# Attention sums of a graph kernel: from float32 products to two float32r products of an exact split

## The reference, cut to what matters

```python
e = leaky_relu(xl[src] + xr[dst], 0.2)
logits = einsum('ehc,hc->eh', e, att)
m = segment_max(logits, dst)
p = exp(logits - m[dst])
denom = segment_sum(p, dst)
out = segment_sum((p / denom[dst])[:, :, None] * xl[src], dst)
x = bn(leaky_relu(out.mean(axis=1) + bias, 0.01) + x)
```

## Time and profile before

| | us |
|---|---|
| median of 3 runs | 5818.48 |
| lowest, highest | 5813.25, 5839.03 |
| profiled execution, its own time | 5812.7 |
| its span, first to last instruction | 5811.0 |
| mean granted TensorE clock, share of full | 0.941 |

### The profile page before, as it was taken

The page is one execution under the profiler, slowest core; times in us unless marked ns, Lnnn a source line. Parts: engine busy times, 40 slices in busy tenths (PEclk is TensorE's granted clock), DMA queues, the critical chain, the costliest instruction groups (busy, mean ns, idle before and its releaser), DMA issues.

```text
span 5811.0 us, 137953 instructions
## 1 busy us (share of the span) xinstructions
PE 5019.3 (86%) x47293; PEld 3476.8 (60%) x47293; DVE 3747.3 (64%) x7195; ACT 1756.4 (30%) x3748; POOL 3820.1 (66%) x3980
## 2 busy tenths in 40 slices
PE   5999999788878888589999985999999859999997
PEld 4777777788868888345555553555555525555555
DVE  6566554888778888556665564566666746556666
ACT  3222222555530000133333322333333233333331
POOL 4777776676637776477777735777777267777770
PEclk8999899899889999899999997999999989999998
DMA  4655554332223333244444432444444234444442
GB/s 115 175 171 166 166 172 143 87 94 84 83 73 93 99 88 88 63 119 125 121 126 126 123 93 65 125 124 123 122 126 126 74 80 126 124 125 126 121 125 63
DMA packets 689966, 663.36 MB, mean 114 GB/s; under 512 B 398323, under 2 KB 480698, under 8 KB 689274
## 3 DMA queue, kind: packets, MB, share of 16 engines
q1 hardware_dynamic: 557482, 489.13, 27.6%
q0 software_dynamic: 127424, 164.72, 13.2%
q10 hardware_dynamic: 4368, 0.70, 0.1%
HBM read 564.89 MB, written 89.17 MB: 113 GB/s over the span
## 4 chain that ended last, share of the span: by engine, by line
PE 57%; issue 16%; POOL 16%; DVE 7%; DVEq 2%; DMA 1%; ACT 1%; ACTq 1%; POOLq 0%
PE ps L1059 18%; PE ps L904 13%; POOL rows L369 11%; PE ps L998 8%; POOL rows L382 5%; PE ps L1019 4%; PE ps L1033 3%; PE ps L919 2%; PE ps L1009 2%; PE ps L984 2%; PE ps L978 1%; DVE acc L1619 1%; DMA rows<-table,idx 1%; DVE region L1782 1%; DVE acc L1807 1%
## 5 line engine op out<-in xcount | busy, mean ns | idle before, releaser
L382 POOL DMA_INDIRECT rows<-table,idx x2340 | 2251.6, 962 | 1108.2 <-issue 710.2
L1059 PE MATMUL ps<-region,hot 128*128 128x272 f32 x4992 | 1314.3, 408 | 171.6 <-DVE region L1760 85.4
L1059 PEld LDWEIGHTS ps<-region,hot 128*128 128x128 f32 x4992 | 916.3, 193 | 466.9 <-issue 291.0
L666 ACT ACTIVATE region<-ps 128x512 f32<-128x512 f32 x1248 | 677.7, 596 | 1674.7 <-PE ps L998 1674.7
L1807 DVE TENSOR_TENSOR acc<-acc,ps 128x272 f32 x1248 | 544.5, 436 | 870.4 <-PE ps L1059 765.9
L904 PE MATMUL ps<-hot,region 128*128 128x192 bf16 (+1 forms) x9216 | 927.5, 261 | 81.1 <-DVE region L1634 56.4
L904 PEld LDWEIGHTS ps<-hot,region 128*128 128x128 bf16 x9216 | 846.5, 104 | 99.4 <-DVE region L1634 61.5
L369 POOL DMA_INDIRECT rows<-table,idx x728 | 699.9, 961 | 259.1 <-issue 221.0
L1782 DVE TENSOR_TENSOR region<-ps,region 128x1056 f32<-128x1056 f32 x582 | 724.9, 1252 | 45.9 <-issue 40.4
L998 PE MATMUL ps<-xT,wcat 64*128 64x512 f32 x2496 | 710.8, 646 | 9.3 <-ACT region L666 9.2
L402 POOL DMA_INDIRECT rows<-table,idx x448 | 429.9, 960 | 206.7 <-issue 120.7
(11 more groups left out here) (304 smaller groups left out, 6470.0 us busy)
## 6 DMA issues: line engine op xcount, KB each, us to landing
hot<-hot_dram SPq DMA_DIRECT2D x624, 256.0 KB
turned<-turned_dram SPq DMA_DIRECT2D x624, 128.0 KB
rows<-table,idx POOLq DMA_INDIRECT x3516
hot_dram<-hot SPq DMA_DIRECT2D x104, 512.0 KB
region<-hot_dram SPq DMA_DIRECT2D x96, 512.0 KB
xwin<-table SPq DMA_DIRECT2D x1664, 24.0 KB
region<-r_dram SPq DMA_DIRECT2D x109, 256.0 KB, 5.9
region<-d_dram SPq DMA_DIRECT2D x104, 256.0 KB
```

What stands on the lines that cost most here:

```text
L382: pool.indirect_dma_start(rows[:, n % 2, j, :], None, table, bass.IndirectOffsetOnAxis(ap=idx[:, s:s + 1], axis=0)).then_inc(rows_in3[n % ...
L666: act.activation(rz[g % 2][:, 2 * t + side, :], ps[:, Z + side, :], ACT.Relu).then_inc(rz_made, 1)
L1059: mm = pe.matmul(ps[:, sum_bank(k, side, i), 0:PC + H], hot[:, b, 4 * side + 2 * i + j, :], px[b][:, 4 * side + 2 * i + j, :], start=(j == ...
```

## The change

For groups below `TAIL` the weighted rows are made in float32 in one buffer `pxf` (the place of the old px[1]). ACT writes them rounded to float32r into `pxh` (`high_half`), DVE subtracts that from pxf and writes the rest to `pxl` (`low_half`), for each side of 128 x 4 x 272. The columns with the maxima are treated alike (`ends_half`; `low_ends` where a chunk begins). PE multiplies `hotr`, a float32r name for the memory of hot, by pxh and by pxl and adds both up in PSUM. pxf, pxh and pxl have one buffer for each side, so weigh of a side now waits for that side's sums of the group before. The last eight groups keep their two float32 buffers and their code. Some semaphores that nothing used are gone, and hot and region1 are placed first in memory; pxh lies where px[0] was, and pxl is a float32r name for the memory of pxf, so the subtraction is in place.

```diff
+        hotr = nc.alloc_sbuf_tensor_at("hotr", [P, 2, 8, P], F32R, offset=hot_at)
+        pxh = nc.alloc_sbuf_tensor_at("pxh", [P, 2, 4, 272], F32R, offset=region1_at)
+        pxl = nc.alloc_sbuf_tensor_at("pxl", [P, 2, 4, 272], F32R, offset=region1_at + 4 * 8 * 272)
...
+        pxh32 = pxh[:, :, :, :].bitcast(F32)
+        pxf = o1[:, 8 * 272:16 * 272].rearrange("p (a j c) -> p a j c", a=2, j=4)
...
+            def ends_half(k, side):
+
+                act.wait_ge(att_summed, 4 * (l * G + k - 1) + 2 * side + 2)
+                act.activation(pxf[:, side, :, PC:PC + H], ends_of(k)[:, side, :, :], ACT.Copy).then_inc(pm_made, 1)
+
+            def high_half(k, side):
+
+                n = PC if k % 8 == 0 else PC + H
+                act.wait_ge(wx_made, 2 * (l * TAIL + k) + side + 1)
+                if k % 8 != 0:
+                    act.wait_ge(pm_made, 2 * (l * G + k) + side + 1)
+                act.activation(pxh[:, side, :, 0:n], pxf[:, side, :, 0:n], ACT.Copy).then_inc(ph_made, 1)
...
                     weights_of(8 * done)
+                    if 8 * done < TAIL:
+                        high_half(8 * done, 0)
                 if u < G:
                     leaky(u, 0)
+                if phase == 2 and 0 <= done < CHUNKS and 8 * done < TAIL:
+                    high_half(8 * done, 1)
                 k = u + 1 - LAG
-                if 0 <= k < G and k % 8 != 0:
+                split = 0 <= k < TAIL and k % 8 != 0
+                if split:
+                    ends_half(k, 0)
+                elif TAIL < k < G:
                     weights_of(k)
                 if u < G:
                     leaky(u, 1)
+                if split:
+                    high_half(k, 0)
...
                     keep(u + 1)
                     turn(u + 1)
+                if split:
+                    ends_half(k, 1)
+                    high_half(k, 1)
...
-                    pe.wait_ge(pm_made, l * G + k + 1)
+                    if k < TAIL and k % 8 == 0:
+                        pe.wait_ge(fl_made, l * (CHUNKS - 1) + k // 8 + 1)
+                    elif k >= TAIL:
+                        pe.wait_ge(pm_made, 2 * (l * G + k) + 2)
...
+                            for part in (pxh, pxl):
+                                mm = pe.matmul(ps[:, sum_bank(k, side, i), 0:PC + H], hotr[:, b, 4 * side + 2 * i + j, :],
+                                               part[:, side, 2 * i + j, :], start=(j == 0 and part is pxh),
+                                               stop=(j == 1 and part is pxl))
...
+                    if k < TAIL and l * G + k > 0:
+                        v.wait_ge(att_summed, 4 * (l * G + k - 1) + 2 * side + 2)
+                    to = pxf[:, side, :, 0:PC] if k < TAIL else px[k % 2][:, 4 * side:4 * side + 4, 0:PC]
...
+                def low_half(k, side):
+
+                    n = PC if k % 8 == 0 else PC + H
+                    v.wait_ge(ph_made, 2 * (l * TAIL + k) + side + 1)
+                    v.tensor_tensor(pxl[:, side, :, 0:n], pxf[:, side, :, 0:n], pxh32[:, side, :, 0:n], ALU.subtract
+                                    ).then_inc(px_made, 1)
...
+                    if phase == 2 and ends and k < TAIL:
+                        low_half(k, 0)
+                        low_ends(k)
+                        low_half(k, 1)
...
                             weigh(k + 1, 0)
                         if windows:
                             add(k, 0, windows)
+                        if 0 <= k + 1 < G:
+                            low_half(k + 1, 0)
                         pick()
                         if 0 <= k + 1 < G:
                             weigh(k + 1, 1)
                         if windows:
                             add(k, 1, windows)
+                        if 0 <= k + 1 < G:
+                            low_half(k + 1, 1)
```

More of the change, by code:

```diff
@@ L24 @@
 F16 = mybir.dt.float16
+F32R = mybir.dt.float32r
 P = 128
@@ L90, in build @@
         hot_dram = nc.dram_tensor("hot_dram", [G, P, 8 * P], F32).ap()
+        hot = sb("hot", [P, 2, 8, P])
+        hot_at = nc.sbuf_base - 4 * 2 * 8 * P
+        region1 = sb("region1", [P, SLOTS * H])
+        region1_at = nc.sbuf_base - 4 * SLOTS * H
+        hotr = nc.alloc_sbuf_tensor_at("hotr", [P, 2, 8, P], F32R, offset=hot_at)
+        pxh = nc.alloc_sbuf_tensor_at("pxh", [P, 2, 4, 272], F32R, offset=region1_at)
+        pxl = nc.alloc_sbuf_tensor_at("pxl", [P, 2, 4, 272], F32R, offset=region1_at + 4 * 8 * 272)
         X = sb("X", [P, W, C])
@@ L284, in build @@
         gathered = [sem(f"gathered{b}") for b in range(3)]
-        rows_in3 = [sem(f"rows_in3_{b}") for b in range(3)]
+        rows_in3 = [sem(f"rows_in3_{b}") for b in range(2)]
         x0_stored, x0_in = sem("x0_stored"), sem("x0_in")
@@ L512, in hot_for @@
                     sp.wait_ge(att_summed, 4 * (l * G + k - 1))
+                to = hotr[:, b, :, :].bitcast(F32) if k < TAIL else hot[:, b, :, :]
                 for half in range(2):
                     at = 512 * (n % 2)
-                    sp.dma_start(hot[:, b, 4 * half:4 * half + 4, :].rearrange("p j n -> p (j n)"),
+                    sp.dma_start(to[:, 4 * half:4 * half + 4, :].rearrange("p j n -> p (j n)"),
                                  hot_dram[8 * c + 4 * half + n // 2, :, at:at + 512]).then_inc(hot_in[b], 16)
@@ L666, in leaky, with ends_of @@
                     act.activation(rz[g % 2][:, 2 * t + side, :], ps[:, Z + side, :], ACT.Relu).then_inc(rz_made, 1)
+            def ends_of(k):
+                n = piece_of(k)
+                return endmax.rearrange("p (j a r) -> p a j r", j=4, a=2)[:, :, :, H * n:H * n + H]
             def weights_of(k):
[L670 to L676, removed]
+                if l * G + k > 0:
+                    act.wait_ge(att_summed, 4 * (l * G + (k - 1 if k > TAIL else k)))
+                to = px[k % 2].rearrange("p (a j) c -> p a j c", a=2) if k >= TAIL else pxh[:, :, :, :]
+                act.activation(to[:, :, :, PC:PC + H], ends_of(k), ACT.Copy).then_inc(pm_made, 2)
+            def ends_half(k, side):
[7 more added lines that the diff above has]
+                act.activation(pxh[:, side, :, 0:n], pxf[:, side, :, 0:n], ACT.Copy).then_inc(ph_made, 1)
             keep(0)
@@ L1058, in sums_half @@
                     for j in range(2):
-                        mm = pe.matmul(ps[:, sum_bank(k, side, i), 0:PC + H], hot[:, b, 4 * side + 2 * i + j, :],
-                                       px[b][:, 4 * side + 2 * i + j, :], start=(j == 0), stop=(j == 1))
+                        if k >= TAIL:
+                            mm = pe.matmul(ps[:, sum_bank(k, side, i), 0:PC + H], hot[:, b, 4 * side + 2 * i + j, :],
+                                           px[b][:, 4 * side + 2 * i + j, :], start=(j == 0), stop=(j == 1))
+                        else:
+                            for part in (pxh, pxl):
+                                mm = pe.matmul(ps[:, sum_bank(k, side, i), 0:PC + H], hotr[:, b, 4 * side + 2 * i + j, :],
+                                               part[:, side, 2 * i + j, :], start=(j == 0 and part is pxh),
+                                               stop=(j == 1 and part is pxl))
                     mm.then_inc(att_summed, 1)
@@ L1783, in weigh, with low_ends @@
                                     xs[:, (k // 8) % 2, k % 8, 4 * side:4 * side + 4, :].unsqueeze(2).broadcast_to([P, 4, H, HK]),
-                                    ALU.mult).then_inc(px_made, 1)
+                                    ALU.mult).then_inc(wx_made if k < TAIL else px_made, 1)
+                def low_half(k, side):
[3 more added lines that the diff above has]
+                                    ).then_inc(px_made, 1)
+                def low_ends(k):
+                    n = piece_of(k)
+                    v.wait_ge(pm_made, 2 * (l * G + k) + 2)
+                    v.tensor_tensor(pxl[:, :, :, PC:PC + H],
+                                    endmax.rearrange("p (j a r) -> p a j r", j=4, a=2)[:, :, :, H * n:H * n + H],
+                                    pxh32[:, :, :, PC:PC + H], ALU.subtract).then_inc(fl_made, 1)
                 def weigh_two(k, side, i):
```

11 lines of the change are left out of this document (6 added, 5 removed).

## The result

The changed kernel takes 6291.36 us (median of 4 runs, 6283.8 to 6300.4) against 5828.75 for the kernel before in the same comparison: a ratio of **1.0803, 95% interval 1.0768 to 1.0838**, or 463 us more. The sign was forecast; the size, 155 us, was a third of it, and the range ended at 6130.

What follows compares the result with a forecast made beforehand. PE was taken as nearly full, with POOL and DVE close behind; after the change, a chain through single buffers. Terms 0.4 + 1.6 + 0 + 2.3 = 4.3 us a chunk, x 36 = +155, gave 5975 us; range 5780 to 6130.

Steps and rivals of the forecast that it cites:

- Prices: Claimed costs of the new instructions: float32r matmul 0.125 us, low half 1.29, high half 1.11; DVE's work 68.2 us a chunk.
- The regular group: Stages 3 to 7 of a chunk: groups of 8.85 and 8.73 us against 8.89 before, gaining next to nothing; +0.4 a chunk.
- The prediction's timetable: A regular group followed from the start of weigh(k+1, 0) through DVE and ACT; the next group starts at 8.85 us.
- a rival at 0.03: PE at 58 of 82 us gets a granted clock of 0.82: +2.6 a chunk more, about 6070 us; chance 0.03.
- The chunk here has short pauses: Argument against the clock rival: the chunk's pauses are short, unlike the start-up window where the clock was 0.82.
- The gathers: POOL's gathers slowed by DVE instructions with two SBUF sources: 3.3 us a chunk more in proportion, or 10.7 at worst.
- The proportion: The 16 low halves, 20.6 us a chunk, lengthen POOL's gathers by 3.3 us a chunk, scaled from today's 1.1.
- half of every hit: Each gather that meets a low half waits half of it: 10.7 us a chunk, POOL needs 86.4; 6120 us, chance 0.10.
- POOL needs 79.0: POOL's need per chunk with gathers slowed in proportion, 79.0 us, below the forecast chunk of 82.4.
- The chain: Weigh, high half, low half, sums, then the same side's next weigh, through single buffers; a chunk of 82.4 us.
- ACT's order: On ACT the high half stands behind leaky(u, 1), so DVE stands still from 2.40 to 3.1 in a regular group.
- the three signs of being wrong: Chunks under 78.1 us, low halves starting without a wait, or the gathers' mean above 1.1 us.

Runs made afterwards that it cites:

- the filled kernel: Changed kernel plus ten products of zeros on PE just before the wait for the pick in stages 2, 4 and 6: 6174.9 us, ratio 1.0610.
- filling wins nothing clear with the pick first: Changed kernel with the pick ahead of the low half, plus six products of zeros ahead of sums_half(k, 1) in stages 2, 4 and 6: 6088.86 us.
- with the pick first: Changed kernel with the pick moved ahead of low_half(k+1, 0) on VectorE, in a regular step and stage 0: 6085.12 us, ratio 1.0452.
- where only PE's work is less: Kernel before, weighted rows below the last eight groups written as float32r and multiplied once, low part left out: 5703.06 us, ratio 0.9795.
- The load alone: Kernel before plus a maximum with two SBUF sources per half group on VectorE: 6089.67 us with the pick behind it, 6082.11 with it ahead.
- the pick first and one SBUF source: Changed kernel, pick ahead, low half replaced by a second weighing, high part counted twice: 5964.17 us, ratio 1.0232.
- The pair of kernels that differ in the added instruction alone: Kernel before, pick ahead of one added VectorE instruction: a maximum with two SBUF sources, 6082.11 us, or a second weighing with one, 5935.2 us.
- one source and two buffers: Kernel before plus a second weighing per half group on VectorE, one source in SBUF, pick ahead of it: 5935.2 us, ratio 1.0187.
- the table: Changed kernel, us above before: two SBUF sources 463 (pick behind), 264 (pick first); low half replaced by a one-source weighing 430 and 142.
- the last experiment: Kernel before, weighted rows below the last eight groups as float32r in two buffers, multiplied once, no split: 5703.06 us, ratio 0.9795.

## Why the prediction was wrong in size

- **Prices: right.** 0.125 us a float32r matmul, 1.29 a low half (1.299; its own row in proportion gives 1.30), 1.11 a high half (1.107), VectorE's work in a chunk 68.2 (66.9).
- **The regular group: the step that failed.** The prediction's timetable has the low half to 4.4 and then, "in every second group the pick (0.9, with the reduction's 0.55), weigh(k+1, 1) to 6.45". So the weighing of side 1 starts as soon as the pick is done, and its wait for sums_half(k, 1) is put at nothing. It can't be nothing: on PE sums_half(k, 1) waits in every even step for that same pick (the semaphore one_picked; the looked-up row and the sums share a PSUM bank), and the change put the pick behind the low half. Before, PE's wait was 85 us in the whole kernel, all of it in stage 2; after, it is 424, the weighing waits 264 for the sums, and the price was 199 us, the difference that moving the pick makes. The prediction counted what the moved pick delays on DVE, and not who waits for it on another engine.
- **The clock: a rival at 0.03, and it happened.** "The chunk here has short pauses" was false, in part because of the first error: PE's pauses before the pick are mostly 3.1 us long, up to 4.1, and the clock in three windows behind them is 0.50. The price, 109 us or more by the filled kernel, is near the 95 that the rival had. That it is a part of the 199 is likely, since filling wins nothing clear with the pick first. Part of the fall isn't the order's: with the pick first the clock is still 0.902, and 0.891 where only PE's work is less.
- **The gathers: the mechanism right, its size between the two ends given.** The proportion gave 3.3 us a chunk and half of every hit 10.7. The load alone lengthened gathers from 962 to 1094 ns, 60 x 0.132 = 7.9 us a chunk. That POOL needs 79.0, with room below 82.4, was therefore the second step that failed: with the pick first it needs some 60 x (1.055 + 0.30) = 81.3, about as long as the chain, and the chunks last 85.2 us in the mean; that the rest comes from two tight partners waiting for each other is argued. The Trainium skill, SBUF — State Buffer, section "Who interferes with whom", says that a VectorE instruction with two inputs in SBUF contends with a GpSimd instruction that reads SBUF, and one with at most one such input, outside the two-port modes, doesn't. The pair of kernels that differ in the added instruction alone agrees: 1094 ns a gather with two inputs in SBUF, 954 with one.
- **The chain: right in length, in part by luck.** 82.4 forecast, 82.1 measured with the pick first and one SBUF source; +155 against +142. But that kernel isn't the one of the timetable: its pick stands ahead of the low half, its clock in that chunk is 0.94 and PE still waits for the pick. ACT's order is not what holds it, and VectorE's time alone, with one source and two buffers, already costs 113.
- **The sum.** 142 (chain) + 122 (gathers, once the order lets them through) + 199 (pick, clock included) = 463. This is one way through the table; by the other the parts are 142, 288 for the pick and 33 for the gathers. The causes overlap, and neither split is the right one.
- **The signs.** None of the three signs of being wrong came: chunks were not under 78.1, the low halves did wait, the gathers' mean stayed at 1.015 us. What failed was a wait that none of them watched.

## What to carry to other kernels

When a step is moved back on one engine, look up every wait of the other engines for it, not only what is queued behind it: here moving one instruction of 0.38 us was worth 199 us. Time put on an engine with room isn't free for that: 576 instructions of 1.25 us cost 113 us, and 148 more when both their sources lay in SBUF and they met the gathers. So compare the same length with another source before blaming the engine's time alone. And before a bound is relieved by adding work elsewhere, relieve it for nothing, as in the last experiment: that says how much there is to win, here 123 us with three quarters of the sums' matmul time gone, before anything is paid for it.

## What the runs showed of the hardware that was not expected

A float32r matmul of 128x272 follows the one before after 0.125 us at 2.4 GHz and 0.23 at 1.2, with its own weight load of 128x128 each time; two of them cost as much as one of the two halves of which a float32 product is made (0.244). Both VectorE and ScalarE wrote float32r in the time that rows with float32 outputs give in proportion: 1.299 us against 1.30, and 1.107 against 1.11. A gather on POOL that starts while a VectorE instruction with two SBUF sources runs can be held up, in the row shown by 1.13 us; one of the same length with a source in PSUM leaves the gathers' mean at 954 ns. And in a chunk in which PE was busy for 72 of 92 us and stood still for 4.11, 3.1 and 3.1 us ahead of three picks, the granted clock was 0.50 in a window behind each of them and 0.83 over the whole.
